# Self-attention of a decoder layer: four key tiles worked in three rounds a step instead of four

## The reference

```python
h = _rms(x, w_ln1)
q = (h @ wq + bq).reshape(B, S, N_HEADS, HEAD_DIM)      # 16 heads of 32
k = (h @ wk + bk).reshape(B, S, N_KV, HEAD_DIM)
v = (h @ wv + bv).reshape(B, S, N_KV, HEAD_DIM)
q, k = _rope(q, k)
scores = jnp.einsum('bqhd,bkhd->bhqk', q, k) * HEAD_DIM ** (-0.5)
causal = jnp.tril(jnp.ones((S, S), bool))
scores = jnp.where(causal[None, None], scores, jnp.finfo(scores.dtype).min)
attn = jax.nn.softmax(scores, axis=-1)
ctx = jnp.einsum('bhqk,bkhd->bqhd', attn, v).reshape(B, S, N_HEADS * HEAD_DIM)
x = x + ctx @ wo
h = _rms(x, w_ln2).reshape(B * S, H)                    # goes to the router and the experts
logits = h @ w_router
```

## Time and profile before

| | us |
|---|---|
| median of three runs | 2413.34 |
| the three runs | 2413.34, 2416.03, 2411.95 |
| span of the profiled execution | 2411.3 |
| self-attention in it, from the first scores of step 0 to the end of step 15 | 1330 to 1730 |

### The profile page before, as it was taken

The page is one execution under the profiler, slowest core; times in us unless marked ns, Lnnn a source line. Parts: engine busy times, 40 slices in busy tenths (PEclk is TensorE's granted clock), DMA queues, the critical chain, the costliest instruction groups (busy, mean ns, idle before and its releaser), DMA issues. The chain is left out here.

```text
span 2411.3 us, 38337 instructions
## 1 busy us (share of the span) xinstructions
PE 2332.4 (97%) x15092; PEld 1496.7 (62%) x15092; DVE 1348.3 (56%) x2103; ACT 1340.7 (56%) x1696; POOL 915.4 (38%) x610
## 2 busy tenths in 40 slices
PE   9999999999999999999999899999899999999998
PEld 7887444444454444444334556666578899998886
DVE  6677544434444434444422656565675578777785
ACT  4333667667766777667897433533522256665222
POOL 2228755565456445555302333333024112221320
PEclk9999999999999999999999999999999999999999
DMA  6003833546344643455532400002045358776431
GB/s 227 18 18 128 284 129 123 189 144 196 124 164 132 217 152 112 147 188 182 171 123 77 146 1 1 19 1 73 19 131 184 118 168 279 268 251 211 145 109 48
DMA packets 203649, 326.67 MB, mean 135 GB/s; under 512 B 69168, under 2 KB 123696, under 8 KB 203312
## 3 DMA queue, kind: packets, MB, share of 16 engines
q1 hardware_dynamic: 184112, 246.50, 30.8%
q0 software_dynamic: 16336, 72.23, 9.1%
q10 hardware_dynamic: 3024, 5.51, 0.7%
HBM read 238.39 MB, written 96.27 MB: 139 GB/s over the span
## 5 line engine op out<-in xcount | busy, mean ns | idle before, releaser
L1115 ACT ACTIVATE A_c_prob<-c_psum 128x1024 f32<-128x1024 f32 x832 | 786.9, 1030 | 274.0 <-PE c_psum L1380 271.6
L1040 POOL TENSOR_TENSOR E_c_roots<-E_c_roots,c_half 128x32 f32<-128x32 f32 (+1 forms) x70 | 361.3, 5164 | 402.2 <-DVE E_c_roots L1132 402.0
L1391 PE MATMUL c_psum<-A_c_prob,c_vq 128*17 128x512 f32 x3328 | 413.0, 596 | 8.7 <-DVE c_oT L1278 8.3
L143 PE MATMUL c_psum<-E_c_w,E_c_c 128*128 128x512 f32 x1248 | 312.0, 399 | 1.4 <-DVEq L1260 0.7
L143 PEld LDWEIGHTS c_psum<-E_c_w,E_c_c 128*128 128x128 f32 x1248 | 226.7, 188 | 122.0 <-issue 41.5
L1380 PE MATMUL c_psum<-c_qq,c_kq 64*128 64x512 f32 x1664 | 285.5, 435 | 12.9 <-ACT A_c_prob L1115 10.2
L1380 PEld LDWEIGHTS c_psum<-c_qq,c_kq 64*128 64x128 f32 x1664 | 135.6, 184 | 155.8 <-ACT A_c_prob L1115 84.0
L1172 DVE COPY E_c_unit<-c_psum 128x256 f32<-128x256 f32 x89 | 37.8, 425 | 328.6 <-PE c_psum L143 328.6
L2787 PE MATMUL m_psum<-A_m_dn_hi,A_m_a 128*128 128x512 f32 (+1 forms) x576 | 187.7, 394 | 1.9 <-DVE A_m_a L2525 1.9
L1391 PEld LDWEIGHTS c_psum<-A_c_prob,c_vq 128*17 128x17 f32 x3328 | 68.6, 96 | 187.7 <-issue 163.8
L143 PE MATMUL m_psum<-R_g_hi,U_s_up 128*128 128x512 f32 x528 | 170.0, 395 | 0.6 <-DVEq L2506 0.6
(11 more groups left out here) (361 smaller groups left out, 3950.4 us busy)
## 6 DMA issues: line engine op xcount, KB each, us to landing
c_kq<-kd SPq DMA_DIRECT2D x120, 416.0 KB, 5.6
kd<-S_c_t SPq DMA_DIRECT2D x96, 256.0 KB, 2.7
E_c_raw<-in_ctxT SPq DMA_DIRECT2D x89, 256.0 KB, 3.1
qd<-A_c_q SPq DMA_DIRECT2D x32, 512.0 KB, 3.9
c_qq<-qd SPq DMA_DIRECT2D x64, 256.0 KB, 3.1
vd<-A_c_vt SPq DMA_DIRECT2D x104, 136.0 KB, 1.8
c_vq<-vd SPq DMA_DIRECT2D x30, 442.0 KB, 4.9
S_up_raw<-in_sup SPq DMA_DIRECT2D x20, 512.0 KB, 5.0
```

What stands on the lines that cost most here:

```text
L143: mm = pe.matmul(out, a(c), b(c), start=first and i == 0, stop=last and i == len(terms) - 1)
L1040: pool.tensor_tensor(rr[:, unit % RB, 0:n], ms[:, unit % RB, 0:n], half[:, 0:n], ALU.pow).then_inc(s_r, 1)
L1115: act.activation(prob[:, t % PB, 2 * (u % 2):2 * (u % 2) + 2, :], score_banks[u % 3], ACT.Exp, scale=XD ** -0.5).then_inc(s_ex, 1)
L1391: mm = pe.matmul(o_bank[32 * j:32 * j + VW, :], vq[:, q % 2, kt, j, :], prob[:, t % PB, j, :], start=kt == 0, stop=kt == CT - 1)
```

## The change

The four key tiles are worked in three rounds: key tile 0; key tiles 1 and 3, which are 384 and 128 columns wide and share the bank (tile 3 from column 384 on); key tile 2. The maxima of the next step are made alike: query tile 3; tiles 2 and 0 side by side; tile 1. DVE still reduces each query tile by itself. ACT takes the exponentials of a round in one instruction, now always into the first half of `pT`; small constants (`ones`, `half` and others) move into the second half.

The items are dealt out anew over the three rounds. Every O but the first of a batch stands in a step with c = 2, the first in the last round of the step with c = 1. V and A share the middle round of steps with c = 0 and 3. H's second half is put ahead of the maxima. R and L move: R0, L0 and R1 into step 15. The spare banks are still taken in turn.

On DVE the O's of a step's last round are now taken behind the reciprocal and the product (`behind`). The diff, cut to its core:

```diff
+ROUNDS = ((0,), (1, 3), (2,))
+MAXIMA = ((3,), (2, 0), (1,))
+NR = len(ROUNDS)
+TOPS = (1, 3, 4)
+BESIDE = T - P
+VALUES = (0, 1, 3, 2)
...
-                a = {0: (0, 2), 1: (0, 1), 2: (0, 1), 3: (0, 1)}[c]
-                if kt in a and n + 2 < self.N:
-                    early.append(self.item("A", n + 2, a.index(kt)))
...
-                if c == 1 and kt == 3 and b:
-                    early += [self.item("O", b - 1, t) for t in range(2)]
-                if c == 2 and kt >= 2 and b:
-                    early.append(self.item("O", b - 1, kt))
...
+                if r < 2 and n + 2 < self.N:
+                    product("A", n + 2, r)
...
+                if n == self.N - 1 and r == 2:
+                    product("R", 1, 0)
+                if c == 1 and r == 2 and b + 1 < B:
+                    for k in range(2, KC):
+                        product("H", b + 1, k)
+                if c == 1 and r == 2 and b:
+                    product("O", b - 1, 0)
+                if c == 2 and b:
+                    product("O", b - 1, r + 1)
+                if n == self.N - 2 and r < 2:
+                    product("G", 0, 2 * r)
+                    late.append(self.item("G", 0, 2 * r + 1))
...
+                for r in range(NR):
+                    act.wait_ge(s_st, n * NR + r + 1)
+                    act.wait_ge(s_pv, n * NR + r)
+                    act.activation(pT[:, 0, :, 0:widths[r]], psum[:, 0:HPC, 0:widths[r]], ACT.Exp, scale=SCALE).then_inc(s_ex, 1)
...
-                dve.reduce_max(topx[:, t // 2, t % 2, ::SD], psum[:, 0:HPC, 0:(t + 1) * P], AX_X).then_inc(s_top, 1)
+                for at, t in zip((0, BESIDE), MAXIMA[r]):
+                    dve.reduce_max(topx[:, t // 2, t % 2, ::SD], psum[:, 0:HPC, at:at + (t + 1) * P], AX_X).then_inc(s_top, 1)
...
+                    if r == NR - 1 and n + 1 < STEPS:
+                        behind = [x for x in items if x.kind == "O"]
+                        for item in items:
+                            if item.kind == "H":
+                                take(item)
+                        maximum(n + 1, r)
+                    else:
+                        if n + 1 < STEPS:
+                            maximum(n + 1, r)
+                        if r == 0 and n:
+                            low_output(n - 1)
+                        for item in items:
                             take(item)
...
-                dve.wait_ge(s_pv, n * TT + TT)
+                dve.wait_ge(s_pv, NR * (n + 1))
                 if n:
                     dve.wait_ge(s_alo, n)
                 if n < STEPS - 1:
                     dve.reciprocal(a[:], sum_bank).then_inc(s_rec, 1)
                     dve.wait_ge(s_rec, n + 1)
                     dve.tensor_tensor(a[:], o_bank, a[:], ALU.mult).then_inc(s_a, 1)
+                for item in behind:
+                    take(item)
...
+            def scores(n, r):
+                p = n % 2
                 for i, (k_part, q_part) in enumerate(((qk_hi, qk_hi), (qk_lo, qk_hi), (qk_hi, qk_lo))):
+                    for at, kt in zip((0, BESIDE), ROUNDS[r]):
+                        for j in range(HPC):
+                            pe.matmul(s_bank[j][:, at:at + T - kt * P], k_part[rows[j], p, 1, kt * P:(kt + 1) * P], q_part[rows[j], p, 0, kt * P:T],
+                                      start=i == 0 and at == 0, stop=False, skip_group_check=True)
```

More of the change, by code:

```diff
@@ L1462, in __init__ @@
         self.items, self.counts, self.spare, self.user = [], {}, 0, {}
-        self.values = [self.item("V", 0, t) for t in range(3)]
+        self.values = [self.item("V", 0, t) for t in VALUES[0:3]]
         self.turn = [self.item("T", 0, 0)]
@@ new lines, in __init__ @@
+                product = lambda kind, at, i: early.append(self.item(kind, at, i))
+                if c == 0 and b and r == 1:
+                    product("V", b, VALUES[2])
+                if c == 3 and r == 1 and b + 1 < B:
+                    product("V", b + 1, VALUES[0])
+                if r < 2 and n + 2 < self.N:
+                    product("A", n + 2, r)
+                if c == 0 and r == 2:
+                    product("V", b, VALUES[3])
+                if c == 3 and r == 2 and b + 1 < B:
+                    product("V", b + 1, VALUES[1])
@@ new lines, in __init__ @@
+                if n == self.N - 1 and r == 0:
+                    product("R", 0, 0)
+                if n == self.N - 1 and r == 1:
+                    for k in range(KC):
+                        product("G", 1, k)
+                    product("L", 0, 0)
+                if n == self.N - 1 and r == 2:
[5 more added lines that the diff above has]
+                    product("O", b - 1, 0)
@@ L1493, in __init__ @@
+                if c == 2 and b:
[3 more added lines that the diff above has]
+                    late.append(self.item("G", 0, 2 * r + 1))
+                if c == 1 and r == 1 and b + 1 < B:
+                    late += [self.item("H", b + 1, k) for k in range(2)]
                 self.early[n].append(early)
@@ L1557, in self_attention @@
         sel = m.sb("sel", [P, P], F32R)
[L1558 to L1563, removed]
+        neg = m.sb("neg", [P, 2, P], BF16)
         unused = pT[:, 1, :, T - P:T]
+        ones = pT[:, 1, 0, 0:SD]
+        half, ss, ms, rr = (pT[:, 1, 0, SD + i * TT:SD + (i + 1) * TT] for i in range(4))
         at = (2 * HPC + 2 * RING - 1) * T
@@ L1737, in _ @@
                     act.activation(wr_hi, wr, ACT.Copy).then_inc(s_wrhi, 1)
[L1738 to L1744, removed]
+                for r in range(NR):
+                    act.wait_ge(s_st, n * NR + r + 1)
+                    act.wait_ge(s_pv, n * NR + r)
+                    act.activation(pT[:, 0, :, 0:widths[r]], psum[:, 0:HPC, 0:widths[r]], ACT.Exp, scale=SCALE).then_inc(s_ex, 1)
+                    if n == 0 and r == 0:
@@ L1752, in _ @@
-                    if c == 2 and kt == 0 and b:
+                    if c == 0 and r == 0 and b >= 2:
+                        normalise("O", b - 2, (2, 3))
+                    if c == 0 and r < 2 and b + 1 < B:
+                        squares("H", b + 1, (2 * r, 2 * r + 1))
+                    if c == 2 and r == 1 and b:
                         squares("O", b - 1, (0, 1))
-                    if c == 3 and kt == 0 and b:
+                    if c == 3 and r == 0 and b:
                         squares("O", b - 1, (2, 3))
-                    for item in line.early[n][kt] + line.late[n][kt]:
+                    for item in line.early[n][r] + line.late[n][r]:
@@ L1847, in _ @@
             dve.memset(topx, 0.0).then_inc(s_zero, 1)
-            for t in reversed(range(TT)):
-                maximum(0, t)
-                if t == TT - 1:
+            for r in range(NR):
+                maximum(0, r)
+                if r == 0:
                     selectors()
@@ L1859, in _ @@
                     dve.tensor_tensor(wr_lo, wr, wr_hi, ALU.subtract).then_inc(s_wr, 1)
[L1860 to L1863, removed]
-                            take(item)
[L1865 to L1873, removed]
+                behind = []
@@ new lines, in _ @@
+                for r in range(NR):
+                    items = line.early[n][r] + line.late[n][r]
+                    if n == STEPS - 1 and r == 1:
+                        mean("O", b - 1)
+                    if r == NR - 1 and n + 1 < STEPS:
[7 more added lines that the diff above has]
+                            maximum(n + 1, r)
+                        if r == 0 and n:
+                            low_output(n - 1)
+                        for item in items:
+                            take(item)
+                    ts = ((0, 1), (2,), (3,))[r]
@@ L2019, in weighted @@
                 mm.then_inc(s_pv, 1)
             put(line.values[0])
-            pe.wait_ge(s_const, 3)
-            maxima(0, TT - 1)
-            put(line.values[1])
-            for t in reversed(range(TT - 1)):
-                pe.wait_ge(s_top, TT - 1 - t)
-                maxima(0, t)
-                if t == TT - 2:
-                    put(line.values[2])
+            pe.wait_ge(s_const, 2)
+            for r in range(NR):
+                if r:
+                    put(line.values[r])
+                    pe.wait_ge(s_top, TOPS[r - 1])
+                maxima(0, r)
@@ L2038, in _ @@
                     elif more:
-                        pe.wait_ge(s_top, (n + 1) * TT + kt)
+                        pe.wait_ge(s_top, (n + 1) * TT + TOPS[r - 1])
                     else:
-                        pe.wait_ge(s_ex, n * TT + kt)
-                    scores(n, kt)
-                    early, late = line.early[n][kt], line.late[n][kt]
-                    parted = early[-1] if more and kt < 2 and early and not late and early[-1].kind in "AV" else None
+                        pe.wait_ge(s_ex, n * NR + r)
+                    scores(n, r)
+                    early, late = line.early[n][r], line.late[n][r]
```

(11 more changed lines are left out.)

146 lines of the change are left out of this document (69 added, 77 removed).

## The result

| | before | after |
|---|---|---|
| median, us | 2414.69 (4 runs, 2411.95 to 2417.84) | 2429.14 (4 runs, 2424.63 to 2434.59) |
| ratio to before, with its 95% interval | | 1.0061 (1.005 to 1.0073) |
| profiled execution: time, span | span 2411.3 | 2428.62, span 2426.9 |
| first scores of step 0 to the experts' first product, span | 428.35 | 443.21 |
| PE's waits in it, added up | 29.05 | 43.63 |

The change makes the kernel slower by 0.6%, 14.5 us by the medians. The profiled executions differ by 15.6 us, and 443.21 - 428.35 = 14.86 us of that lie between the first scores of step 0 and the first product of the experts (the line that writes `m_psum` first, at 1773.86 after and 1758.69 before). The last row of the table comes from rows of 3.4 us width set side by side from 1320 to 1775 us: each gives the mean granted clock c, and (1 - c) x 2 of its width was at 1.2 GHz.

What follows compares the result with a forecast made beforehand. PE was taken to bound the kernel, with its own work plus its waits. Terms -12.8 - 14.0 + 4.9 + 19.8 + 3.6 = +1.5 us, plus 9 for the clock, took span 2411.3 to 2421.8, median 2424; range 2411 to 2432.

Steps and rivals of the forecast that it cites:

- the side named at 0.75: Whole kernel: slower than 2418.2 us, chance 0.75.
- The merged round: Self-attention, key tiles 1 and 3 in one round: saves 0.8 us a step, 12.8 us in 16 steps.
- The waits: PE in self-attention: waits that go -14.0 us, with H +4.9, O's behind the reciprocal +19.8, steps 14 and 15 about +0.8.
- The six stalls: Ends of steps 5, 6, 9, 10, 13, 14: PE waits 3.3 us each for an O behind the reciprocal, 19.8 us.
- H's waits: Steps 1, 5, 9: 0.7 us each; 1.0 more in 5 and 9, 0.8 more in step 1; 4.9 us together.
- those of the end: Waits of 2.6 and 1.9 us in step 14, 2.4 and 0.9 in step 15, 3.8 in the tail.
- The clock: Self-attention: eight new drops to 1.2 GHz, two of the present three gone; six more at 1.5 us, 9 us.
- The rival in which the stalls weigh more: Each stall costs 1.7 us more, the end of the part another 2: 2430 us and above, chance 0.15.
- The rival in which the clock holds: The clock holds or falls as seldom as before the change: 2415 us, chance 0.16.
- I see no other order in its stream: DVE at a step's last round: no order was seen that has the O ready sooner, which would mean no stalls.
- the largest term: The O behind the reciprocal on DVE: PE stalls 3.3 us at six places, 19.8 us.
- R1: Moved from the tail into step 15: 2.8 us of product added there, nothing won in the tail.

Runs made afterwards that it cites:

- the filled stall: The changed kernel, with PE doing 22 useless transposes into a free bank ahead of each of six waits for an O's bank: 2418.80 us, ratio 1.0022.
- the first experiment: The changed kernel, with DVE taking the O's of a step's last round ahead of the reciprocal again: 2402.42 us, ratio 0.995.
- The last two kernels: The first experiment (2402.42 us), with R1 in step 15, and the same kernel with R1 put back in the tail behind the last O (2397.29 us).

## Why the prediction was right

Forecast 2424, measured 2429.14, within the range of 2411 to 2432 and on the side named at 0.75. Point by point:

**The merged round: right.** 0.8 us a step were taken, 12.8 in all; the table gives 11.7 to 12.4. In step 8 the rows show it where it was looked for:

```profile
1534.34 0.51 PE L2030 MATMUL s_psum<-Q_s_qk 32*128 32x384 f32 x8
...
1536.06 0.47 PE L143 MATMUL s_psum<-R_s_hi,S_s_h 128*128 128x512 f32 x1
...
1540.95 0.61 PE L2018 MATMUL s_psum<-s_neg,ident 128*128 128x256 bf16 x4
...
1543.80 0.72 PE L143 MATMUL s_psum<-S_s_h,R_s_hi 128*128 128x512 f32 x2
```

The scores of both key tiles take 1.72 us (1.12 + 0.81 before), maxima and weighting 2.85 (2.13 + 1.27): 0.21 + 0.55 = 0.76 us. In the scores the masks stay as eight matmuls (`128x128 ... x8`), as said. For the maxima the two masks of a bank have become one of 256 columns (L2018), which the forecast hadn't counted.

**The waits: right in sum.** PE's idle time was to change by -14.0 + 4.9 + 19.8 + 0.8, and by 2.8 for the tail's wait that R1 no longer covers: +14.3 us, of which 1.1 us of gain lie ahead of step 0, so +15.4 in the stretch of the table. It rose by 43.63 - 29.05 = 14.6. The six stalls were 3.06 or 3.07 us, not 3.3. From the reciprocal's start DVE needs 5.39 us instead of 5.50 (the first addition starts 0.08 us before the product has ended), and PE comes to the bank 2.37 us behind that start instead of 2.19. H's waits came where they were worked out: 0.61 us in steps 1, 5 and 9 (0.7), 0.9 us more in 5 and 9 (1.0), and in step 1 the transposes waited 1.25 us, 0.8 more than the 0.42 at the end of step 5 (0.8). So did those of the end:

```profile
1697.06 0.66 PE L1996 MATMUL s_psum<-ident,R_s_in 128*128 128x128 f32 x4 [2.52 <-DVE X L1837]
...
1709.03 0.66 PE L1996 MATMUL s_psum<-ident,R_s_in 128*128 128x128 f32 x4 [1.92 <-DVE X L1837]
...
1730.73 1.31 PE L1996 MATMUL s_psum<-ident,R_s_in 128*128 128x128 f32 x8 [2.45 <-DVE R_g_lo L1841]
...
1732.95 0.61 PE L2006 MATMUL s_psum<-ident,U_s_turned 16*128 16x16 f32 x4 [0.91 <-DVE R_g_lo L1841]
...
1760.77 3.65 PE L2106 MATMUL s_psum<-ident,A_s_xs 128*128 128x128 f32 x16 [3.80 <-ACT A_s_xs L1707]
```

against 2.6, 1.9, 2.4, 0.9 and 3.8 us.

**The clock: right in kind, too small in size.** Nine drops were forecast (the three of before, less two, and eight new ones) and eight came, not all where they were put: behind the sixth stall, 3.06 us in step 15, the clock held, and the 2.45 us wait ten microseconds on brought one instead. The price of a drop of 3.4 us, 1.5 us, is what the filled stall measured. What was too small is the term "six more, at 1.5 us, 9 us": it counts each drop as a single stretch, and three were double. That makes eleven stretches of 3.4 us against three, eight more and not six: 38 us at half clock against 10, or 12 us. The rival in which the stalls weigh more had named this, though its own sum is off: 1.7 us more at six stalls and 2 at the end are 12 us, not the 6 that it adds. The rival in which the clock holds is refuted by the filled stall: of the 26.7 us that the O's place is worth, some 9 are the clock's.

**The rest of the miss** is no step of the sum. The forecast went from a span of 2411.3 to 2421.8, and 2426.9 came: 3 us are the clock; another 2 lie outside self-attention, 1.58 us of them ahead of it (in after's profile it begins at 1317.73 instead of 1316.15), in a part that the change doesn't touch. Its runs spread by 10 us, so the 5 us between forecast and median are not more than one execution differs from the next.

**"I see no other order in its stream" was wrong.** The sentence stands in the largest term. The order was there: behind the last reduction and ahead of the reciprocal, where the kernel before takes the O's of its steps with c = 2. It holds the reciprocal up by 1.3 us, for which there is room. Nothing in the forecast of the change hung on it, but it hid a version that is 26.7 us faster.

**R1: right in kind, too small in size.** Its move was put at a loss of 2.8 us. Undoing it in the first experiment's kernel gave back 5.1: 2.1 us of waits, and 3.0 of clock.

## What to carry to other kernels

When two engines trade buffers in a fixed rotation, ask of each slow instruction which buffer release stands behind it: a release that is ready goes ahead of a long operation whose own result is wanted later. A stall of the engine that sets the pace costs its length and then the clock, here half as much again; filling it with useless work gives the second part back and tells the two apart in one run. And when a change bundles a restructuring with a reordering, undo the reordering alone before judging the restructuring: here the reordering was worth +26.7 us and the restructuring -12.3.

## What the runs showed of the hardware

- **Whether a wait of 2 to 2.5 us brings a drop differs between executions.** The last two kernels run the same instructions up to the end of step 14. With R1 in step 15, the second of step 14's waits of 2.52 and 1.91 us was followed by half clock; with R1 in the tail the same waits, of 2.52 and 1.92 us, were not. In the kernel after it was the first of the two, and with the filled stall neither. The stretches behind the second, with R1 in step 15 and then with R1 in the tail:

```profile
1687.20:1690.60 3.40, 3.40 (x10) 2.68 (x9) 0.00 (x0) 0.51 (x1) 0.00 (x0) 0.58 0.00 0
```

```profile
1687.80:1691.20 3.40, 3.18 (x32) 1.81 (x30) 1.17 (x2) 0.00 (x0) 0.00 (x0) 1.00 0.00 0
```

  A forecast of drops at waits of this size can only be a count, not a list of places. Whether much of the spread of the runs (10 us after, 5 us with the O's ahead) comes from it was not tried; the runs of the kernel before, which has no waits of this size in this part, spread by 7.6 us.
- **Filler holds the clock**: 22 fp32 transposes of 128 columns, 2.57 us, in a stall of 3.07 us, with 0.65 us left idle. No drop followed at six such places, where five had.
- **A reciprocal takes about five times as long on DVE as a product or an addition of its size** here: 3.35 us for 128 x 512 from PSUM, beside 0.69 us for the product and for each addition; the longest other operation of this size in the part has a mean of 0.95. It is worth knowing which instruction of a stream is the one that nothing should queue behind.
